# Starting the first batch's key projection on pieces of the context, with new engine orders, in a gated cross-attention and quantised feed-forward kernel

## The chip, the cores and the metric

The kernel runs on one core of one Trainium2 chip. The metric is the device time of one execution in microseconds. The kernel before takes 1027.44 us (median of 3 runs, 1027.41 to 1028.69).

## The reference

Sixteen batches of 224 rows of width 512 attend to 750 context rows of width 384 each, with 8 heads of 64, and then go through a quantised feed-forward layer of width 2048. All of it is in float32:

```python
h   = layernorm(x)
q, k, v = h @ W_q, context @ W_k, context @ W_v
sim = q k^T * 64**-0.5, masked keys set to the lowest float
x   = x + tanh(g_xattn) * (softmax(sim) @ v @ W_o + b_o)
z   = layernorm(x)
ffn(z): y = bitlinear(gelu(bitlinear(z, w1, b1)), w2, b2)
bitlinear(x, w, b) = act_quant(rmsnorm(x)) @ weight_quant(w).T + b
act_quant:    s = 127 / max|row|;  round(x s), clipped, / s
weight_quant: s = 1 / mean|w|;     round(w s) clipped to -1..1, / s
x   = x + tanh(g_ffn) * ffn(z)
```

The scale of each feed-forward weight is the mean of its absolute values, so no element of w2 or w1 can be quantised before all eight pieces of that matrix have been read and summed.

## The kernel before, in words

**Number formats.** A projection (keys, queries, values, output) is carried in float16 pairs: every operand is split into a high part (a cast) and a low part (the rest), and a product is three matmuls per contraction tile of 128 rows, high by high, low by high and high by low (`split_product`, line 770). ScalarE writes the high part of each result from PSUM and VectorE the low part. The feed-forward layer uses 8-bit weights.

**Banks.** PSUM has four banks for scores and `RING = 4` banks (`ps_g`) that all other products share in turn. The product with turn n goes to bank n % 4 and first waits (`need_bank`) until the product four turns before it has been emptied by its last reader, for keys the low part on VectorE.

**Orders by hand.** Each engine and the SyncE DMA queue works through a written list of steps, `SP_SEQ`, `PE_SEQ`, `ACT_SEQ`, `DVE_SEQ` and `POOL_SEQ` (lines 78 to 334). A step is `kind:n:batch`. An engine does its list strictly in order, and steps wait for each other through semaphores. The kinds that the text speaks of:

- `LX`, `LC`, `LM`, `LR` (SP): loads of a batch's x rows, of one third of its context (128 of 384 contraction rows by 750 keys), of its mask, and of residual rows of one tile. `LM` of a batch waits until the mask of the batch before has been turned into a bias (`MB`, POOL, line 1317).
- `PD`/`PW`: load of W_k, W_q, W_v, W_o (n = 0 to 3), then high part (ACT, line 1137) and low part (DVE, line 931). DVE's part releases TensorE through `wready`.
- `N1`, `XN`, `XH`: layer norm of x: statistics (DVE, lines 1013 and 1017), inverse root (POOL, lines 1323 and 1326), subtraction of the mean (DVE, line 1021, one instruction for each half of 112 rows), high part (ACT, line 1193) and low part (DVE, line 1025). `XT` is the DMA that transposes a half for the query projection.
- `CX`: high part (ACT, line 1199) and low part (POOL, line 1310) of one third of the context. The semaphore `ctx_lo` counts the low parts.
- `K:n` (PE, line 842): 8 key groups a batch, head pair n // 2, key half n % 2: 9 matmuls of 375 columns, 3 for each third. It begins after all three thirds: `need(pe, "ctx_lo", b, KC - 1)`. ACT copies (line 1174), DVE's `KL` (line 1000). `Q`, `V`: query and value groups, `QL`, `VL` on DVE.
- `S:n`: scores of 128 of the 896 rows; then for two units each `M` (DVE, mask and row minimum, line 978), `E` (ACT, exponential, line 1157), `R` (DVE), `N` (ACT, division, line 1162), `H` and `L` (POOL, casts, lines 1301 and 1306), `T` (transpose by DMA), `PV` (PE, line 826).
- `WL`, `WA`, `WS`, `WM`, `WB`, `WQ`: the feed-forward weights, 16 pieces: load, sum of absolute values (ACT, line 1147), their sum (DVE, line 958), the sum over partitions (PE, line 783, and DVE, line 947), scaling (POOL, line 1290), clipping (DVE, line 965). Pieces 0 to 7 are w2, 8 to 15 w1. This work is spread over the first 140 us.
- `O`, `L2`, `L3`, `L4`, `XQ`, `F1`, `GE`, `GS`, `GM`, `G2`, `G3`, `HT`, `F2`: output projection and feed-forward layer of a 128-row tile.

For batch 0 the lists of before begin like this:

```
PE   K:0 K:1 K:2 K:3 Q:0 Q:1 S:0 V:0 Q:2 S:1 K:4 K:5 S:2 V:1 V:2 V:3 S:3 K:6 V:4 V:5 K:7 S:4 Q:3 WM:0 S:5
ACT  PW:0 CX:0 CX:1 XH:0 CX:2 XH:1 PW:1 PW:2 K:0 K:1 K:2 K:3 Q:0 WA:0 Q:1 WA:1 E:0
DVE  N1 PW:0 XN XH:0 XH:1 PW:1 KL:0 KL:1 PW:2 QL:0 KL:2 KL:3 QL:1 M:0 M:1
POOL N1 CX:0 CX:1 CX:2 MB H:0 H:1 L:0 L:1
SP   PD:0 LX LC:0 LC:1 LC:2 PD:1 PD:2 XT:0 WL:0 XT:1 LM WL:1 WL:3 LM(batch 1) WL:5 LX(batch 1) ...
```

Of the kernel before, what the change touches and what calls it, by code (L numbers as in the profile page):

```python
# [17 lines left out]
HT = TQ // 2  # L18
# [3 lines left out]
CH = J // 2  # L22
# [50 lines left out]
def in_order(text):  # L73
# [10 lines left out]
    LC:2:3 XT:1:3 T:1:2 T:0:2 T:3:2 XQ:0:1 T:2:2 LC:1:4 T:4:2 LC:0:4 T:5:2 F2:1:0 LM:0:3 XQ:1:1 T:6:2 LR:1:2 T:7:2
    T:8:2 HT:0:1 T:9:2 LR:0:2 T:11:2 T:12:2 T:10:2 T:13:2 HT:1:1 LC:2:4 T:0:3 LX:0:5 F2:0:1 T:1:3 XT:1:4 XT:0:4
    XQ:0:2 F2:1:1 T:2:3 T:3:3 LR:0:3 T:4:3 T:6:3 LM:0:4 T:5:3 XQ:1:2 T:7:3 T:8:3 T:9:3 LC:0:5 HT:0:2 LR:1:3 T:11:3
    LC:1:5 T:12:3 T:10:3 T:13:3 LC:2:5 LX:0:6 XT:0:5 LM:0:5 XT:1:5 F2:0:2 HT:1:2 T:0:4 XQ:0:3 T:2:4 T:1:4 LR:1:4
    T:3:4 T:4:4 XQ:1:3 F2:1:2 T:5:4 T:6:4 T:7:4 HT:0:3 LC:1:6 T:8:4 LC:0:6 T:9:4 T:10:4 T:11:4 LX:0:7 T:13:4 T:12:4
# [15 lines left out]
    T:2:13 LM:0:14 T:3:13 T:4:13 F2:1:11 XQ:1:12 T:5:13 LR:1:13 LC:0:15 T:6:13 T:7:13 T:9:13 T:8:13 LM:0:15 T:11:13
    T:10:13 T:12:13 T:13:13 XT:0:15 HT:1:12 LC:2:15 T:0:14 T:1:14 F2:1:12 T:2:14 T:3:14 XQ:0:13 T:5:14 T:4:14
    XT:1:15 T:6:14 LR:0:14 T:7:14 XQ:1:13 HT:0:13 T:8:14 T:9:14 LR:1:14 T:11:14 T:10:14 T:13:14 T:12:14 F2:0:13
    LR:0:15 T:0:15 T:1:15 T:2:15 HT:1:13 T:3:15 XQ:0:14 T:4:15 F2:1:13 T:5:15 T:6:15 T:7:15 T:8:15 LR:1:15 T:9:15
    T:10:15 HT:0:14 T:11:15 T:12:15 T:13:15 F2:1:14 F2:0:14 F2:0:15 F2:1:15
# [351 lines left out]
def build(nc, x_d, ctx_d, mask_d, gx_d, gf_d, wq_d, wk_d, wv_d, wo_d, bo_d, w1_d, b1_d, w2_d, b2_d, out_d):  # L460
    with ExitStack() as stack:
# [937 lines left out]
```

## Time and profile before

| | |
|---|---|
| median of 3 runs | 1027.44 us |
| the profiled execution | 1028.62 us, of which its span (first to last instruction) 1026.7 us |
| TensorE (PE) busy | 977.3 us, 95% |
| ScalarE (ACT), VectorE (DVE), GpSimd (POOL) busy | 860.0, 800.2, 779.3 us |
| DMA queue of SyncE | 83.5% of 16 engines' span |
| mean granted TensorE clock | 0.989 |

The profile counts an engine as busy while it executes. A matmul's end is modelled, so TensorE's busy time is not the time at its peak, but its idle time is time in which it had nothing it could start. A timeline row gives start, length, engine, source line, operation, what it writes and reads, how many instructions are merged, and in brackets the idle time of the engine just before with what released it.

### The profile page before, as it was taken

To read this page: it belongs to the slowest core of one execution; us is meant where nothing else is said; L and a number is where in the kernel's file an instruction comes from. 1 tells how busy PE (TensorE), PEld (TensorE's weight loads), DVE (VectorE), ACT (ScalarE), POOL (GpSimd) and SP (SyncE) were. 2 spreads that over 40 slices of the span, in tenths; PEclk is the share of its full clock that TensorE was granted. 3 is DMA by queue.
4 is the path that set the end of the run, shared out by engine and by line. 5 is a ranking of instruction groups with operands and counts; after the bars stand their busy time and mean duration, and the time that the engine had idled before them with its cause. 6 is when DMAs were issued, how large, how long until landed. Compare 5 with 4: busy or idle time off the path is not lost.

```text
span 1026.7 us, 25406 instructions
## 1 busy us (share of the span) xinstructions
PE 977.3 (95%) x9216; PEld 562.0 (55%) x9216; DVE 800.2 (78%) x1870; ACT 860.0 (84%) x1386; POOL 779.3 (76%) x739
## 2 busy tenths in 40 slices
PE   3979898999999999999999999999999999999887
PEld 2536555565555656555555555555565556556443
DVE  6669788868998677977769778877868776876766
ACT  4879777988879879897888889798897977889866
POOL 3599998787678787877678696877687688867861
PEclk9989999999999999999999999999999999999989
DMA  6999979997879988978879798897888888778961
GB/s 229 239 212 244 206 159 157 177 163 135 189 142 173 187 168 157 169 130 172 155 153 172 157 187 162 137 174 142 169 163 182 166 167 153 138 133 162 168 100 41
DMA packets 472331, 169.10 MB, mean 165 GB/s; under 512 B 450320, under 2 KB 452368, under 8 KB 471824
## 3 DMA queue, kind: packets, MB, share of 16 engines
q1 hardware_dynamic: 472208, 167.48, 83.5%
q8 instruction: 75, 1.23, 0.5%
q14 instruction: 48, 0.39, 0.1%
HBM read 48.28 MB, written 7.34 MB: 54 GB/s over the span
## 4 chain that ended last, share of the span: by engine, by line
PE 68%; DVE 9%; POOL 6%; ACT 6%; DMA 5%; issue 4%; SPq 1%; DVEq 0%; POOLq 0%; ACTq 0%
PE ps_g L776 38%; PE ps_g L826 9%; PE ps_s L809 8%; PE ps_g L864 8%; PE ps_g L901 5%; POOL p L1306 3%; DMA pt<-p 2%; DVE xa L1021 2%; DVE prob L978 1%; POOL ctx L1310 1%; POOL p L1301 1%; ACT prob L1157 1%; ACT prob L1162 1%; DVE xc L1047 1%; ACT h_sb L1255 1%
## 5 line engine op out<-in xcount | busy, mean ns | idle before, releaser
L1306 POOL TENSOR_TENSOR p<-prob,p 128x750 f16<-128x750 f32 x224 | 357.8, 1608 | 4.8
L1301 POOL CAST p<-prob 128x750 f16<-128x750 f32 x224 | 186.0, 835 | 125.7 <-ACT prob L1162 100.1
L978 DVE CUSTOM_DVE_ANT_0 prob<-ps_s,mbias 128x750 f32<-128x750 f32 x224 | 205.8, 933 | 51.3 <-PE ps_s L809 35.2
L1157 ACT ACTIVATE prob<-prob,rmin 128x750 f32<-128x750 f32 x224 | 204.5, 914 | 26.2 <-DVE rmin L978 25.3
L1162 ACT ACTIVATE prob<-prob,rrec 128x750 f32<-128x750 f32 x224 | 198.7, 914 | 29.5 <-DVE rrec L923 29.3
L776 PE MATMUL ps_g<-ctx,wk 128*128 128x375 f16 x1152 | 201.1, 327 | 18.1 <-POOL ctx L1310 17.4
L776 PE MATMUL ps_g<-wv,ctx 128*128 128x512 f16 (+1 forms) x864 | 198.3, 379 | 1.2 <-DVE k_sb L1000 0.6
L776 PEld LDWEIGHTS ps_g<-ctx,wk 128*128 128x128 f16 x1152 | 110.9, 99 | 100.9 <-issue 29.6
L776 PEld LDWEIGHTS ps_g<-wv,ctx 128*128 128x128 f16 (+1 forms) x864 | 86.4, 103 | 97.3 <-issue 6.5
L809 PE MATMUL ps_s<-k_sb,q_sb 64*32 64x375 f16 (+2 forms) x2688 | 129.4, 325 | 7.7 <-DVE k_sb L1000 4.4
L826 PE MATMUL ps_g<-pt,v_sb 128*64 128x224 f16 (+2 forms) x2448 | 121.6, 256 | 4.5 <-DMA pt<-p 4.1
L826 PEld LDWEIGHTS ps_g<-pt,v_sb 128*64 128x64 f16 x2448 | 109.3, 111 | 23.0 <-issue 16.6
L864 PE MATMUL ps_g<-w,xqt 128*128 128x512 fp8e4 x432 | 103.6, 384 | 3.6 <-ACT xqt L1218 2.0
L901 PE MATMUL ps_g<-w,hqt 128*128 128x512 fp8e4 x432 | 97.7, 379 | 3.1 <-DMA hqt<-hq 2.4
L809 PEld LDWEIGHTS ps_s<-k_sb,q_sb 64*32 64x32 f16 (+2 forms) x2688 | 62.4, 95 | 65.5 <-issue 40.2
L1310 POOL TENSOR_TENSOR ctx<-ctx_f,ctx 128x750 f16<-128x750 f32 x47 | 74.1, 1585 | 17.8 <-ACT ctx L1199 17.3
L1075 DVE SCALAR_TENSOR_TENSOR h_sb<-ps_g,sm,b 128x512 f32<-128x512 f32 x108 | 76.8, 744 | 11.3 <-PE ps_g L864 10.7
L994 DVE SCALAR_TENSOR_TENSOR v_sb<-ps_g,v_sb 128x512 f16<-128x512 f32 x96 | 64.9, 685 | 24.3 <-ACT v_sb L1187 23.9
L776 PE MATMUL ps_g<-xt,wq 128*128 128x224 f16 x768 | 82.1, 259 | 0.7 <-DVE wv L931 0.4
L1000 DVE SCALAR_TENSOR_TENSOR k_sb<-ps_g,k_sb 128x375 f16<-128x375 f32 x128 | 67.8, 542 | 18.2 <-ACT k_sb L1174 18.0
L776 PEld LDWEIGHTS ps_g<-xt,wq 128*128 128x128 f16 x768 | 71.9, 98 | 12.9 <-issue 5.3
L776 PE MATMUL ps_g<-wo,attn 128*128 128x512 f16 x336 | 76.7, 380 | 1.3 <-DVE attn L988 1.3
(129 smaller groups left out, 1328.6 us busy)
## 6 DMA issues: line engine op xcount, KB each, us to landing
ctx_f<-in_ctx SPq DMA_DIRECT2D x47, 375.0 KB, 4.0
xa<-in_x SPq DMA_DIRECT2D x16, 448.0 KB, 4.7
xr<-in_x SPq DMA_DIRECT2D x28, 256.0 KB, 3.4
out<-xr SPq DMA_DIRECT2D x28, 256.0 KB, 2.9
pt<-p SPq DMA_TRANSPOSE x254, 4.1
h_sb<-in_w SPq DMA_DIRECT2D x4, 512.0 KB, 5.7
w<-in_w SPq DMA_DIRECT2D x3, 512.0 KB, 6.1
xr<-in_w SPq DMA_DIRECT2D x3, 512.0 KB, 5.0
```

The costliest lines, as they stand in the source:

```text
L776: mm = nc.tensor.matmul(out, lhs, rhs, start=(m == 0), stop=(m == len(steps) - 1))
L809: mm = nc.tensor.matmul(ps_s[at:at + width, e, c, 0:CH], q_sb[rows, j, qa, q:q + width], k_sb[rows, j, ka, c * CH:(c + 1) * CH], start=(m ...
L826: mm = nc.tensor.matmul(g[e * DH:(e + 1) * DH, 0:size], v_sb[:, p, t, va, (2 * j + e) * DH:(2 * j + e + 1) * DH], pt[:, e, pa * NT + t, pl ...
L864: mm = nc.tensor.matmul(g[:, :], xqt_t[:, k, :], w1v[:, k, f * 512:(f + 1) * 512], start=(k == 0), stop=(k == KD - 1))
L901: mm = nc.tensor.matmul(g[:, :], hqt_t[:, k, :], w2v[:, k, :], start=(k == 0), stop=(k == KF - 1))
L978: nc.vector.tensor_tensor_reduce(prob[:, (b * NU + n) % PROBS, :].rearrange("p (c k) -> p c k", c=2), ps_s[:, n % 2, :, 0:CH], mbias[:, :] ...
L1075: nc.vector.scalar_tensor_tensor(out=h_t[:, f * 512:(f + 1) * 512], in0=g[:, :], scalar=sm2[:, t % 2, 4:5], in1=b1[:, f * 512:(f + 1) * 51 ...
L1157: nc.scalar.activation(prob[:, (b * NU + n) % PROBS, :], prob[:, (b * NU + n) % PROBS, :], ACT.Exp, bias=rmin[:, n:n + 1], scale=-1.0, acc ...
L1162: nc.scalar.activation(held, held, ACT.Copy, scale=rrec[:, n:n + 1]).then_inc(normed, 1)
L1301: nc.gpsimd.tensor_copy(p16[:, u % HILO, 0, 0:J], prob[:, u % PROBS, :]).then_inc(hi_pool, 1)
L1306: nc.gpsimd.tensor_tensor(p16[:, u % HILO, 1, 0:J], prob[:, u % PROBS, :], p16[:, u % HILO, 0, 0:J], ALU.subtract).then_inc(lo_pool, 1)
L1310: nc.gpsimd.tensor_tensor(ctx[:, 1, n, :], ctx_place(b * KC + n), ctx[:, 0, n, :], ALU.subtract)\
```

## The change

Three things change.

**1. Key groups 0 to 3 of batch 0.** `K:0` now waits for one third of the context at a time. For the first two thirds it issues that third's three matmuls for each of the four groups, each into its own bank, and for the last third those of group 0. `K:1` to `K:3` issue the last third's three matmuls of their group. Number and shapes of the matmuls are as before.

```diff
+                elif kind == "K" and b == 0 and n < RING:
+
+                    for k in range(KC) if n == 0 else (KC - 1,):
+                        if n == 0:
+                            need(pe, "ctx_lo", b, k)
+                        for m in (n,) if k == KC - 1 else range(RING):
+                            j, c2 = m // 2, m % 2
+                            for a, c in ((0, 0), (1, 0), (0, 1)):
+                                mm = nc.tensor.matmul(bank(kind, m, b)[:, 0:CH], wk[:, a, k, j * 128:(j + 1) * 128],
+                                                      ctx[:, c, k, c2 * CH:(c2 + 1) * CH], start=(k == a == c == 0),
+                                                      stop=(k == KC - 1 and c == 1))
+                    mm.then_inc(s["k_proj"], 1)
```

**2. Two waits on VectorE**, both in the first feed-forward tile (t = 0):

```diff
                     need_tile(dve, "xq", t - 1)
+                    if t == 0:
+                        dve.wait_ge(w_abs, 2 * NW)
                     nc.vector.tensor_scalar(xc[:, :], xr_t, mv2[:, c, 0:1], None, ALU.subtract)\
...
                     need_tile(dve, "x2_amp", t)
+                    if t == 0:
+                        need(dve, "w_mean", 0, 1)
                     nc.vector.tensor_scalar(sm2[:, c, 4:5], sm2[:, c, 3:4], 1.0 / (QMAX * UNIT * W_UNIT), wmean[:, 0:1],
```

The first is there because `WA` writes its scratch output over `xc`, which `L2` writes.

**3. All five lists** have the same steps in another order: 371 of 464 places hold another step in SP's, 386 of 654 in PE's, 857 of 1035 in ACT's, 872 of 1071 in DVE's and 505 of 656 in POOL's, in every batch. For batch 0 they now begin:

```diff
-PE   K:0 K:1 K:2 K:3 Q:0 Q:1 S:0 V:0 Q:2 S:1 K:4 K:5 S:2 V:1 V:2 V:3 S:3 K:6 V:4 V:5 K:7 S:4 Q:3 WM:0 S:5
+PE   K:0 K:1 K:2 K:3 Q:0 Q:1 S:0 Q:2 V:0 S:1 K:4 K:5 S:2 V:1 V:2 V:3 K:6 V:4 V:5 K:7 S:3 S:4 Q:3 WM:0 S:5
-ACT  PW:0 CX:0 CX:1 XH:0 CX:2 XH:1 PW:1 PW:2 K:0 K:1 K:2 K:3 Q:0 WA:0 Q:1 WA:1 E:0
+ACT  PW:0 CX:0 XH:0 XH:1 CX:1 CX:2 PW:1 K:0 K:1 PW:2 K:2 K:3 Q:0 WA:0 Q:1 WA:1 E:0
-DVE  N1 PW:0 XN XH:0 XH:1 PW:1 KL:0 KL:1 PW:2 QL:0 KL:2 KL:3 QL:1 M:0 M:1
+DVE  PW:0 N1 XN XH:0 XH:1 PW:1 KL:0 KL:1 KL:2 KL:3 QL:0 PW:2 M:0 M:1 QL:1
-POOL N1 CX:0 CX:1 CX:2 MB H:0 H:1 L:0 L:1
+POOL CX:0 N1 CX:1 CX:2 MB H:0 L:0 H:1 L:1
-SP   PD:0 LX LC:0 LC:1 LC:2 PD:1 PD:2 XT:0 WL:0 XT:1 LM WL:1 WL:3 LM' WL:5 LX' LC:0' WL:2 LC:1' WL:7 T:0 WL:4 T:1 WL:6
+SP   PD:0 LX LC:0 LC:1 LM LC:2 PD:1 PD:2 XT:0 XT:1 WL:0 WL:1 LM' WL:2 LX' WL:5 WL:3 PD:3 WL:7 WL:4 LC:0' T:0 LC:1' WL:6 T:1
```

(a prime marks a step of batch 1). Where the sum of w2's absolute values is awaited and batch 1 begins:

```diff
-ACT  ... N:5 WA:4 WA:5 E:6 K:6 CX:0' K:7 WA:6 V:4 WA:7 XH:0' Q:3 XH:1' V:5 CX:1' E:7 E:8 E:9 CX:2'
+ACT  ... N:5 V:5 CX:0' WA:5 CX:1' WA:6 WA:7 E:6 E:7 K:7 Q:3 XH:1' CX:2' E:8 E:9
-DVE  ... KL:6 VL:4 WS:0 M:8 WM:0 XH:0' XH:1' M:9 QL:3 VL:5 KL:7
+DVE  ... KL:6 M:8 WS:0 M:9 WM:0 R:3 QL:3 XH:0' KL:7 XH:1'
-POOL ... CX:0' L:5 WB:0 CX:1' WB:1 CX:2' H:6 WB:2 WB:3 L:6
+POOL ... CX:0' H:5 CX:1' L:5 WB:0 WB:1 CX:2' WB:2 H:6 L:6
```

Around the new waits DVE's list read `O:1 QL:3 WS:1 L2:1 WM:1 R:3 M:8` and reads `O:1 L2:1 R:3 QL:3 WS:1 WM:1 KL:0 M:8`.

## Rows read from the trace of the kernel before

**Rows 1.** Stretches of the whole run: busy us (instructions) by engine, granted clock, DMA
```profile
core 0: us, PE busy (x) PEld busy (x) DVE busy (x) ACT busy (x) POOL busy (x), PEclk, DMA share, GB/s
0.00:50.00 50.00, 33.80 (x270) 18.73 (x270) 33.31 (x57) 33.58 (x56) 24.06 (x30) 1.00 0.84 235
50.00:62.00 12.00, 4.36 (x67) 2.45 (x64) 7.27 (x21) 12.00 (x21) 10.62 (x8) 0.76 0.92 227
62.00:108.00 46.00, 45.53 (x438) 27.94 (x436) 38.18 (x78) 38.13 (x75) 45.56 (x36) 0.95 1.03 228
108.00:162.00 54.00, 47.78 (x506) 29.20 (x504) 45.93 (x104) 41.64 (x74) 50.52 (x45) 1.00 0.90 171
162.00:960.00 798.00, 793.07 (x7450) 456.50 (x7451) 629.71 (x1510) 687.48 (x1094) 615.59 (x588) 1.00 0.86 161
960.00:1027.00 67.00, 52.76 (x494) 27.18 (x492) 45.78 (x103) 47.19 (x70) 32.97 (x37) 0.91 0.46 91
```

**Rows 2.** Timeline of all engines from 5 to 31 us (start, length)
```profile
5.32 1.48 ACT L1137 ACTIVATE wk<-xr 128x1536 f16<-128x1536 f32 x1 [3.32 <-DMA xr<-in_wk]
6.81 1.29 DVE L1013 BATCH_NORM_STATS2 st<-xa 112x6 f32<-112x512 f32 x2 [5.96 <-DMA xa<-in_x]
7.65 1.80 ACT L1199 ACTIVATE ctx<-ctx_f 128x750 f16<-128x750 f32 x2 [0.84 <-DMA ctx_f<-in_ctx]
...
8.23 1.73 DVE L931 SCALAR_TENSOR_TENSOR wk<-xr,wk 128x1536 f16<-128x1536 f32 x1
8.40 1.60 POOL L1323 TENSOR_SCALAR ve<-mv 112x2 f32<-112x2 f32 x1 [4.92 <-DVE mv L1017]
9.87 6.05 DVE L1021 TENSOR_SCALAR xa<-xa,mv 112x512 f32<-112x512 f32 x2
...
10.90 3.17 POOL L1310 TENSOR_TENSOR ctx<-ctx_f,ctx 128x750 f16<-128x750 f32 x2
...
15.79 7.31 PE L776 MATMUL ps_g<-ctx,wk 128*128 128x375 f16 x36 [15.79 <-POOL ctx L1310]
...
15.96 0.72 ACT L1193 ACTIVATE xh<-xa,rs 112x512 f16<-112x512 f32 x1 [3.48 <-DVE xa L1021]
...
16.59 1.89 ACT L1137 ACTIVATE wq<-h_sb 128x2048 f16<-128x2048 f32 x1
...
18.51 2.29 DVE L931 SCALAR_TENSOR_TENSOR wq<-h_sb,wq 128x2048 f16<-128x2048 f32 x1 [1.05 <-ACT wq L1137]
18.56 4.15 PEld L776 LDWEIGHTS ps_g<-ctx,wk 128*128 128x128 f16 x26 [0.17 <-issue]
...
19.76 0.98 ACT L1174 ACTIVATE k_sb<-ps_g 128x375 f16<-128x375 f32 x2
...
20.72 1.00 DVE L1000 SCALAR_TENSOR_TENSOR k_sb<-ps_g,k_sb 128x375 f16<-128x375 f32 x2
...
23.51 2.46 PE L776 MATMUL ps_g<-xt,wq 128*128 128x224 f16 x24 [0.41 <-DVE wv L931]
...
25.90 1.13 PE L809 MATMUL ps_s<-k_sb,q_sb 64*128 64x375 f16 x12
...
26.39 0.83 POOL L1317 TENSOR_SCALAR mbias<-mask 128x750 bf16<-128x750 uint8 x1 [10.75 <-DMA mask<-in_mask]
...
30.52 0.57 ACT L1187 ACTIVATE v_sb<-ps_g 128x512 f16<-128x512 f32 x1
```

**Rows 3.** Timeline of TensorE from 52 to 67 us
```profile
53.74 0.38 PE L783 MATMUL ps_g<-wsum,xqt 128*128 128x1 f32 x2 [1.93 <-DVE wsum L958]
58.51 2.08 PE L809 MATMUL ps_s<-k_sb,q_sb 64*32 64x375 f16 x48 [4.39 <-DVE k_sb L1000]
61.74 5.34 PE L776 MATMUL ps_g<-ctx,wk 128*128 128x375 f16 x18 [1.15 <-POOL ctx L1310]
```

**Rows 4.** Line 1021 from 100 to 1000 us: ns of one, min/median/max
```profile
L1021 DVE TENSOR_SCALAR xa<-xa,mv x26: 474/943/3606, 149.7 to 853.7; 112x512 f32<-112x512 f32 x26
```

**Rows 5.** DMA issues from 18.5 to 19.8 us, us from issue to landing
```profile
xt<-xh SPq DMA_TRANSPOSE x1, 4.8
```

**Rows 6.** The page's costliest groups: the exponential, busy us, mean ns
```profile
L1157 ACT ACTIVATE prob<-prob,rmin 128x750 f32<-128x750 f32 x224 | 204.5, 914 | 26.2 <-DVE rmin L978 25.3
```

More of the change, by code:

```diff
@@ L84 @@
[L84 to L88, printed above, removed]
@@ L104 @@
[L104 to L108, printed above, removed]
+    PD:0:0 LX:0:0 LC:0:0 LC:1:0 LM:0:0 LC:2:0 PD:1:0 PD:2:0 XT:0:0 XT:1:0 WL:0:0 WL:1:0 LM:0:1 WL:2:0 LX:0:1 WL:5:0
@@ new lines @@
+    T:2:11 T:3:11 LR:0:11 LC:1:13 LC:0:13 XQ:1:10 T:4:11 T:5:11 T:6:11 T:7:11 T:8:11 T:9:11 HT:0:10 T:10:11 T:11:11
+    T:12:11 T:13:11 LX:0:14 XT:0:13 LR:1:11 LM:0:13 XT:1:13 LC:2:13 T:0:12 T:1:12 T:2:12 HT:1:10 XQ:0:11 T:4:12
+    F2:0:10 T:3:12 T:5:12 XQ:1:11 T:7:12 LC:1:14 LR:1:12 T:8:12 T:6:12 LC:0:14 T:9:12 HT:0:11 T:10:12 T:11:12
+    T:13:12 T:12:12 LX:0:15 LC:2:14 LM:0:14 HT:1:11 T:0:13 T:1:13 F2:1:10 T:2:13 XT:1:14 T:3:13 XT:0:14 T:5:13
+    T:4:13 T:6:13 XQ:1:12 T:7:13 T:8:13 LC:0:15 F2:0:11 T:9:13 LR:1:13 T:10:13 F2:1:11 T:11:13 T:12:13 T:13:13
@@ L147 @@
[L147 to L151 removed]
+    K:0:0 K:1:0 K:2:0 K:3:0 Q:0:0 Q:1:0 S:0:0 Q:2:0 V:0:0 S:1:0 K:4:0 K:5:0 S:2:0 V:1:0 V:2:0 V:3:0 K:6:0 V:4:0
@@ new lines @@
+    N:12:2 N:13:2 GE:1:1 PL:1:2 V:4:3 E:0:3 K:5:3 K:6:3 GS:1:1 E:1:3 V:5:3 XH:0:4 XH:1:4 K:7:3 N:0:3 N:1:3 CX:0:4
+    CX:1:4 E:2:3 G3:1:1 E:3:3 PL:2:2 PL:3:2 N:2:3 N:3:3 Q:3:3 CX:2:4 E:4:3 E:5:3 E:6:3 E:7:3 N:4:3 N:5:3 L4:0:2
+    E:8:3 Q:0:4 V:0:4 V:1:4 E:9:3 N:6:3 N:7:3 N:8:3 GE:0:2 E:10:3 K:0:4 L4:1:2 K:1:4 K:2:4 N:9:3 E:11:3 PL:0:3
+    GS:0:2 K:3:4 V:2:4 E:12:3 N:10:3 V:3:4 E:13:3 Q:1:4 K:4:4 G3:0:2 N:11:3 N:12:3 N:13:3 E:0:4 E:1:4 K:5:4 PL:1:3
+    XH:0:5 GE:1:2 N:0:4 V:4:4 N:1:4 K:6:4 XH:1:5 K:7:4 CX:0:5 CX:1:5 V:5:4 Q:2:4 E:2:4 E:3:4 N:2:4 PL:2:3 PL:3:3
@@ new lines @@
+    PL:1:10 V:4:11 N:0:11 E:2:11 V:5:11 CX:0:12 K:6:11 GS:1:9 K:7:11 E:3:11 N:1:11 N:2:11 N:3:11 CX:1:12 PL:2:10
+    PL:3:10 CX:2:12 Q:2:11 G3:1:9 E:4:11 Q:3:11 K:0:12 E:5:11 N:4:11 L4:0:10 E:6:11 E:7:11 V:0:12 N:5:11 E:8:11
+    E:9:11 N:6:11 L4:1:10 N:7:11 K:1:12 N:8:11 GE:0:10 V:1:12 V:2:12 GS:0:10 XH:0:13 XH:1:13 Q:0:12 Q:1:12 K:2:12
+    E:10:11 PL:0:11 E:11:11 V:3:12 N:9:11 N:10:11 K:3:12 K:4:12 N:11:11 K:5:12 G3:0:10 E:12:11 E:13:11 N:12:11
+    N:13:11 E:0:12 E:1:12 PL:1:11 V:4:12 GE:1:10 N:0:12 V:5:12 N:1:12 K:6:12 GS:1:10 K:7:12 Q:2:12 Q:3:12 E:2:12
@@ new lines @@
+    F1:5:10 R:6:11 M:0:12 M:1:12 F1:6:10 R:0:12 F1:7:10 M:2:12 M:3:12 PA:1:11 VL:4:12 VL:5:12 XH:0:13 XH:1:13
+    KL:6:12 KL:7:12 QL:2:12 QL:3:12 M:4:12 M:5:12 R:1:12 GM:1:10 M:6:12 PA:2:11 PA:3:11 G2:1:10 R:2:12 F2:0:10
+    N1:0:14 O:0:11 L2:0:11 O:1:11 QL:0:13 M:7:12 L3:0:11 XN:0:14 R:3:12 L2:1:11 VL:0:13 QL:1:13 KL:0:13 M:8:12
+    M:9:12 F2:1:10 L3:1:11 F1:0:11 F1:1:11 R:4:12 F1:2:11 KL:1:13 F1:3:11 PA:0:12 M:10:12 M:11:12 GM:0:11 G2:0:11
+    KL:2:13 M:12:12 KL:3:13 R:5:12 M:13:12 VL:1:13 VL:2:13 VL:3:13 R:6:12 KL:4:13 M:0:13 F1:4:11 F1:5:11 F1:6:11
@@ L334 @@
+    L:4:15 XB:0:15 L:5:15 H:6:15 H:7:15 L:6:15 H:8:15 L2:1:14 L:7:15 L:8:15 H:9:15 L:9:15 G2:0:14 H:10:15 H:11:15
+    L:10:15 L3:1:14 L:11:15 H:12:15 H:13:15 L:12:15 L:13:15 L2:0:15 XB:1:15 G2:1:14 L2:1:15 G2:0:15 G2:1:15 L3:0:15
+    L3:1:15
 """)
```

457 lines of the change are left out of this document (221 added, 236 removed).

## The prediction

> **What bounds the kernel now.** I first read the stretches of the whole run [rows 1], because every list changes and the question is where TensorE can still be given time. TensorE is the bound: over the 798 us from 162 to 960 us it is idle for 798.00 - 793.07 = 4.9 us in all, at full clock, and no other engine is near that. Its idle time is at the two ends: 16.2 us up to 50 us, 7.6 us from 50 to 62, 0.5 us from 62 to 108, 6.2 us from 108 to 162, and about 14 us after 960. So time that is won before 62 us is kept only if the stretch from 62 to 162 lets it through. From 62 to 108 TensorE has no slack, so it passes a lead on if its inputs come earlier too. But GpSimd is full there (45.56 of 46 us) and so is the DMA (share 1.03), so a lead of TensorE alone would become a wait.
>
> Then I read the timeline of the start [rows 2]. TensorE waits 15.79 us, for GpSimd's low part of the last third of the context. The 36 key matmuls take 7.31 us from there. Of their 36 weight loads 26 come from 18.56 on in 4.15 us, 0.16 us apart; the 10 before them took 2.8 us, about 0.31 apart after the first pair. That is 375 columns at 1.2 and then at 2.4 GHz, after an engine that had done nothing so far (the granted clock's column says 1.00 for the whole stretch, so here I go by the spacing). The other chain of the start is x: the two mean subtractions take 6.05 us together. Then come both high parts, W_q's split, and the first query group at 23.51. Scores follow at 25.90, and the row minimum waits for the mask's bias, which GpSimd writes at 26.39 after 10.75 us of waiting for a mask load that stood late in the DMA list.
>
> Third, the stall at 50 to 62 [rows 3]. TensorE waits 1.93 us for the sum of w2's absolute values, 4.39 for a key group's low part queued behind other work on ScalarE and VectorE, 1.15 for batch 1's context. ScalarE is busy 12.00 of the 12 us [rows 1], so this stall is a matter of what stands ahead of what on ScalarE. TensorE's clock falls in it: 0.76 for the stretch, and the next 18 key matmuls take 5.34 us where 18 take half of about 5.9 us at full clock.
>
> **Part 1: the start.** Removed: the wait for all three thirds. Walking the new lists with the durations of [rows 2]:
> - VectorE has W_k's low part first: ready at 6.80, 1.64 us (the row less the overlap), done 8.45. Statistics 1.29 + 0.2: done 9.95.
> - GpSimd has the first third first: its high part is there at 8.46, 1.6 us, done 10.1. TensorE can start at 10.1 instead of 15.8.
> - Mean subtractions from 9.95. Before, they took 6.05 us while GpSimd was at work without a pause from 8.40 to 15.65; elsewhere one takes 0.47 to 3.61 us, median 0.94 [rows 4]. Now GpSimd has two small instructions and then nothing until ScalarE gives it the second third, which stands behind both `XH`. So I take 1.6 us for the pair. Bounds: 0.9 and the old 6.05.
> - Both `XH` on ScalarE (0.72 each) from 11.5 to 12.9, then both `CX` (0.9 each): 13.8 and 14.6. GpSimd: second third 13.7 to 15.3, last third to 16.9. That is 1.2 us later than before for the last third, the price of putting x first.
> - TensorE: 12 matmuls from 10.1, cold for the most part, 3.5 us, done 13.6; wait to 15.3; 12 at 0.16 to 17.3; 12 to 19.2. Bounds for the last 24: 0.16 each (3.8 us) or 0.31 each (7.4 us) if the pause costs the clock. I take the first, because in [rows 3] the pauses before the clock fell were longer (1.93 and 4.39 us).
> - x transposes: first at 13.0, second issued by 14.4, landing 4.8 us later [rows 5]: 19.2.
> - W_q: ScalarE 14.6 to 16.5, VectorE 2.29 from 16.9 (it waits for GpSimd's last third, see below): 19.2. Before: 20.80. Key low parts 0.5 each after it, so bank 0 is free at 19.7 and `Q:0` starts there, 3.8 us earlier than 23.51. ScalarE puts W_v's high part (three quarters of 1.89, 1.4 us) ahead of `K:2`, and VectorE does four `KL` before `QL:0`: done 22.3. `S:0` then starts at 22.3 instead of 25.90: 3.6 us earlier.
> - The mask's load moves ahead of `LC:2`. It delays the last third's load by one issue, about 0.5 us, which `XH` covers, since `CX:2` now runs at 13.7. The bias is ready long before `S:0`, and the next batch's mask load, x load and five weight loads, queued behind that bias at 27.2, go out some 6 us sooner.
>
> From here to the stall TensorE has work without gaps, and of its order little but the place of `S:3` differs, so the lead is **3.6 us** if ScalarE and VectorE empty the banks as before.
>
> For the mean subtractions the trace shows this too: GpSimd's variance instruction of 2 columns took 1.60 us during VectorE's W_k split [rows 2]. The Trainium skill (SBUF — State Buffer, Who interferes with whom) has it that VectorE's two-port modes, and VectorE instructions with two SBUF inputs, share a port pair with GpSimd under an exclusive lock. The trace agrees with 1.60 and 6.05 us. By that rule the pair of subtractions would cost about 1 us once GpSimd idles, 0.6 less than I take, and the start of `XH` would move by as much; the sum does not use it.
>
> **Part 2: the stall at 50 to 62.** ScalarE's list up to `WA:7` has the same steps as before less `E:6` and `K:7`, plus `V:5`, `XH:0` and `CX:1` of batch 1: -0.91 [rows 6] -0.49 +0.57 +0.72 +0.9 [rows 2] = +0.8 us. So `WA:7` and TensorE's `WM:0` come 3.6 - 0.8 = 2.8 us earlier. Loads do not hold it, as they go out sooner. Behind it stand `E:6 E:7 K:7 Q:3` (0.91 + 0.91 + 0.49 and, for 224 columns, some 0.4: 2.7 us), then VectorE's `QL:3`, `XH:0`, `KL:7` (0.4, 0.7 and 0.5 like their high parts): `KL:7` ends 4.3 us after `WA:7`. Before it was 4.9 (53.6, just ahead of `WM:0`, to 58.5 [rows 3]). `S:5` is 3.4 us earlier. Batch 1's last third: GpSimd had `WB CX WB CX` after the mean and has `WB WB CX`, one subtraction of 1.6 us less. So `K:0` of batch 1 starts 2.8 + 1.6 = 4.4 us earlier, at 57.3. **Lead 4.3 us** at the end of the stall, for TensorE and for GpSimd alike, so the full stretch up to 108 can pass it on. The low clock stays, since the wait before `S:5` is nearly as long as before.
>
> **Part 3: 62 to 162.** The same steps, GpSimd still full. One thing helps: `CX:2` of batch 2 stands one `L` earlier. One thing can hurt: DVE's `L2:1` now waits for `WA:15`, with `R:3` and `QL:3` behind it. But `QL:3` needs ScalarE's `Q:3`, which itself stands behind `WA:15`, and `R:3` is late by one weight sum at most. I cost it at nothing; what hides it is ScalarE's order. If that cover failed, N:6 and through it GpSimd would be late by about 1.5 us once. The wait for `w_mean` is met long before. Value 0, bounds -3 (half of the 6.2 us idle) and +2 (half of the lead lost).
>
> **Part 4: the other 13 batches.** At most 4.9 us of idle to gain in 800 us, so every reordering there can only lose more than it gains. No row shows what a new order does. Bounds: -2, and +4, if as much idle again is made as there is now. I take 0, near the present state.
>
> **Part 5: the last 67 us**, 14 us idle, mostly waits of the last two tiles, whose order in PE's list is nearly the same. Value 0, bounds -1.5 and +1.5.
>
> **Sum.** -4.3, rounded to -4.2 for a start that hangs on several landings. Against the profiled execution's own 1028.62 that is 1024.4. That execution is 1.2 us above the median of the three runs, so against 1027.44 the forecast is **1023.2 us**.
>
> **The rivals.**
> - *A, the forecast* (0.50): the lead of 4.3 us goes through. 1021.3 to 1025.3.
> - *B, the pieces bring little* (0.12). Either the pause of 1.7 us costs the clock (24 matmuls by 0.15 = 3.7 us), or the subtractions stay long and hold `XH` and with it `CX:1` on ScalarE, which is now behind them (4.4 us). The key groups then end at about 23, and only the GpSimd order of part 2 is left of the gain: 1027.44 - 0.8 = 1026.6. For it: the 6.05 us. Against it: GpSimd is idle then.
>  The Trainium skill (TensorE: Matmul & The Clock Gate, Part 1) says that the array's clock halves after idleness and recovers only after sustained work. This trace agrees at 15.79 and at 58.51. By that rule the pause alone could give B; the 0.12 comes from the lengths of the pauses in [rows 3], not from it.
> - *C, the lead is half absorbed* (0.15) between 62 and 162, where DMA and GpSimd are full. For it: both at capacity. Against: both start their share earlier. 1027.44 - 2 = 1025.4.
> - *D, the new orders also close gaps* (0.14): 3 us of the 6.2 and 1 of the 4.9. 1019.2.
> - *E, slower* (0.09): lists in the steady state that hold TensorE. Places moved furthest are `XH:1` of batch 12 (25 and 28 places earlier on ScalarE and VectorE), where ScalarE waits in order for the layer norm and the free transpose buffer, and exponentials queue behind. The steady part has 13 batches; at 0.5 us more idle in each it costs 6.5 us, more than the lead, and gives 1029.7. It decides once idle from 162 to 960 passes 4.9 + 4.3 = 9.2 us.
>
> **How the numbers follow.** About 2 us, 0.2%, is what a measurement of this kernel tells from no change: faster is below 1025.4, slower above 1029.5. Faster: nearly all of A, D, half of C: 0.71. Same: the rest of C, B: 0.20. Slower: E: 0.09. The range 1019.0 to 1027.6 holds A, B, C and part of D, and leaves out E and the far part of D.
>
> **What would show it.** Key matmuls at about 10.1, in three groups with a pause before the second; both subtractions under 2.5 us; `Q:0` near 19.7; `S:0` near 22.3; `WM:0` near 51; batch 1's keys near 57.3; TensorE's idle from 162 on near 5 us again. The forecast is wrong if the lead at batch 1's keys is under 2 us (part 1 or 2), or if it is there and idle after it has grown (parts 3 to 5).

## The result: slower, and where the time went

The changed kernel takes **1036.14 us** (median of 4 runs, 1034.13 to 1036.61), the kernel before 1027.43 beside it (4 runs, 1027.35 to 1028.69): the ratio is 1.007, 95% interval 1.0053 to 1.0086. The forecast was 1023.2 with a range to 1027.6. So the change costs some 9 us where a gain of 4 was expected. The profiled execution took 1036.61, of which the span is 1034.8 us.

I read the same stretches first as before the change. Stretches of the changed kernel, columns as in [rows 1]:

```profile
0.00:50.00 50.00, 33.63 (x258) 18.22 (x258) 32.02 (x57) 35.20 (x59) 25.85 (x31) 1.00 0.91 254
50.00:62.00 12.00, 7.44 (x81) 4.53 (x82) 9.92 (x25) 11.80 (x20) 11.26 (x8) 0.57 0.99 224
62.00:108.00 46.00, 41.68 (x379) 24.80 (x379) 33.51 (x65) 32.00 (x62) 37.96 (x31) 0.89 0.78 188
108.00:162.00 54.00, 50.79 (x530) 31.14 (x528) 47.91 (x108) 43.69 (x77) 52.50 (x46) 1.00 0.95 183
162.00:960.00 798.00, 786.82 (x7407) 454.24 (x7402) 629.73 (x1497) 684.77 (x1094) 614.53 (x584) 1.00 0.85 160
960.00:1027.00 67.00, 56.99 (x550) 29.39 (x548) 52.56 (x121) 51.70 (x76) 38.95 (x43) 0.92 0.55 104
```

Two rows stand out. From 62 to 108 us GpSimd is busy 37.96 us where it had 45.56 [rows 1]: the full stretch that was to pass the lead on has holes in it. And from 162 to 960 TensorE is idle 798.00 - 786.82 = **11.2 us** where it was 4.9. The prediction named 9.2 us as the point from which rival E decides.

Then I set both executions side by side at equal work: for each of TensorE's steps its start now less its start before. This is worked out from the two timelines:

```
step (start before, us)      start now less start before, us
first key group  (15.8)      -5.1
S:0              (25.9)      -3.5
at 43                        -3.7
at 52                        +0.1
K:0 of batch 1   (61.7)      -1.7
at 79                        -1.5
at 90                        +4.4
at 238                       +1.2
at 288                       +5.9
at 440                       +7.6
at 956                       +9.1
```

The start did what it was to do. Most of the loss is made in four stretches: 43 to 52, 79 to 90, 238 to 288 and 288 to 440. Between the second and the third, 3.2 us of it come back. The timeline of the start, changed kernel:

```profile
10.31 0.87 DVE L1033 TENSOR_SCALAR xa<-xa,mv 112x512 f32<-112x512 f32 x2
10.65 3.77 PE L845 MATMUL ps_g<-ctx,wk 128*128 128x375 f16 x12 [10.65 <-POOL ctx L1326]
15.65 4.00 PE L845 MATMUL ps_g<-ctx,wk 128*128 128x375 f16 x24 [1.24 <-POOL ctx L1326]
19.88 2.46 PE L776 MATMUL ps_g<-xt,wq 128*128 128x224 f16 x24 [0.22 <-issue]
22.36 0.81 PE L809 MATMUL ps_s<-k_sb,q_sb 64*128 64x375 f16 x8
```

The keys start at 10.65 (forecast 10.1), the query at 19.88 (19.7) and the scores at 22.36 (22.3). Now the four stretches. TensorE of the changed kernel, the rows that end a long wait (in brackets its length and what ended it):

```profile
45.55 1.61 PE L776 MATMUL ps_g<-ctx,wk 128*128 128x375 f16 x9 [2.48 <-DVE v_sb L1006]
...
50.25 1.14 PE L809 MATMUL ps_s<-k_sb,q_sb 64*128 64x375 f16 x12 [2.01 <-DVE rmin L990]
...
56.40 2.08 PE L809 MATMUL ps_s<-k_sb,q_sb 64*32 64x375 f16 x48 [2.71 <-DVE k_sb L1012]
60.08 2.35 PE L776 MATMUL ps_g<-ctx,wk 128*128 128x375 f16 x7 [1.60 <-POOL ctx L1326]
...
84.64 1.61 PE L776 MATMUL ps_g<-ctx,wk 128*128 128x375 f16 x9
90.56 3.00 PE L776 MATMUL ps_g<-ctx,wk 128*128 128x375 f16 x9 [4.32 <-DVE v_sb L1006]
...
275.61 1.74 PE L776 MATMUL ps_g<-ctx,wk 128*128 128x375 f16 x9 [3.04 <-DVE k_sb L1012]
...
429.74 0.60 PE L876 MATMUL ps_g<-w,xqt 128*128 128x512 fp8e4 x2 [1.51 <-DVE xr L1139]
```

At 45.55, 90.56, 275.61 and 429.74 TensorE waits for VectorE to empty a bank. The wait at 90.56 costs its clock too: nine matmuls take 3.00 us where the nine before took 1.61, and the granted clock of the stretch is 0.89. What VectorE does just before is a mean subtraction (`XN`, now line 1033), and before 429.74 the layer norm's centring (`L2`, line 1061). VectorE of the changed kernel in the four places:

```profile
39.92 4.97 DVE L1033 TENSOR_SCALAR xa<-xa,mv 112x512 f32<-112x512 f32 x2
44.81 1.27 DVE L1006 SCALAR_TENSOR_TENSOR v_sb<-ps_g,v_sb 128x512 f16<-128x512 f32 x2
...
83.48 4.71 DVE L1033 TENSOR_SCALAR xa<-xa,mv 112x512 f32<-112x512 f32 x2
...
268.44 6.33 DVE L1033 TENSOR_SCALAR xa<-xa,mv 112x512 f32<-112x512 f32 x2
...
424.11 2.98 DVE L1061 TENSOR_SCALAR xc<-xr,mv 128x512 f32<-128x512 f32 x1
```

A pair takes 4.97, 4.71 and 6.33 us; at 10.31 it took 0.87, and there GpSimd had only the last 0.2 us of a context third and two small instructions of 2 columns. GpSimd at the same times, changed kernel:

```profile
41.14 3.08 POOL L1322 TENSOR_TENSOR p<-prob,p 128x750 f16<-128x750 f32 x2
...
84.84 3.07 POOL L1322 TENSOR_TENSOR p<-prob,p 128x750 f16<-128x750 f32 x2
...
269.46 4.63 POOL L1322 TENSOR_TENSOR p<-prob,p 128x750 f16<-128x750 f32 x3
...
423.63 3.18 POOL L1322 TENSOR_TENSOR p<-prob,p 128x750 f16<-128x750 f32 x2
```

GpSimd's instructions there end at 44.22, 87.91, 274.09 and 426.81 us. Each time the one instruction that was held ends 0.28 us later; the other subtraction of the pair takes 0.47 to 0.73. This is theory **P** (port): a subtraction that meets GpSimd at work is held, here through one to three more of GpSimd's instructions, and behind it in VectorE's list stands the eviction that frees TensorE's next bank. At 429.74 the chain is longer (the centring, then a maximum and a row minimum before the eviction), and no run tested this place in the changed orders.

Not every subtraction is held so long. Of the 64 in the two profiles 57 meet a GpSimd instruction that is running. 50 of these wait at most for that one instruction (49 end 0.28 to 0.35 us after it, one before it) and take at most 1.83 us, even where GpSimd's next one follows without a pause:

```profile
149.74 1.59 DVE L1033 TENSOR_SCALAR xa<-xa,mv 112x512 f32<-112x512 f32 x1
```
```profile
149.53 1.51 POOL L1322 TENSOR_TENSOR p<-prob,p 128x750 f16<-128x750 f32 x1
150.99 1.01 POOL L1317 CAST p<-prob 128x750 f16<-128x750 f32 x1
```

The subtraction ends at 151.33, inside GpSimd's run. The other seven are passed over by one to three more GpSimd instructions and take 1.57 to 5.94 us. What decides between the two is open.

The old order had long pairs too, in other places (6.05 us at the start, where TensorE waited for the context anyway), and the sum over all 32 is nearly equal, 39.7 us before and 40.4 now. So no table of busy time shows it; only the place does.

For line 1033 from 100 to 1000 us the median is 1026 ns and the longest 5937, where [rows 4] has 943 and 3606:

```profile
L1033 DVE TENSOR_SCALAR xa<-xa,mv x26: 473/1026/5937, 149.7 to 854.3; 112x512 f32<-112x512 f32 x26
```

### The profile page after: what moved, and what is told of

Read it like the earlier page. It is cut to its first block, busy times and chain, and to the rows that moved or that the text cites. A ratio compares the mean times of both kernels' runs of the same rounds, so it can differ in the third digit from the quotient of the medians.

```text
span 1034.8 us, 25408 instructions
## 1 busy us (share of the span) xinstructions
PE 981.5 (95%) x9216; PEld 564.2 (55%) x9216; DVE 807.2 (78%) x1870; ACT 861.1 (83%) x1386; POOL 781.0 (75%) x739
## 4 chain that ended last, share of the span: by engine, by line
PE 64%; DVE 11%; POOL 9%; ACT 7%; issue 5%; DMA 3%; SPq 1%; DVEq 0%; POOLq 0%; ACTq 0%
PE ps_g L776 35%; PE ps_s L809 8%; PE ps_g L826 7%; PE ps_g L876 7%; PE ps_g L913 6%; POOL p L1322 3%; POOL p L1317 2%; DVE xa L1033 2%; POOL ctx L1326 2%; ACT prob L1173 2%; DVE prob L990 1%; DVE xc L1061 1%; DMA pt<-p 1%; ACT prob L1178 1%; SPq L740 1%
## 5 line engine op out<-in xcount | busy, mean ns | idle before, releaser
L776 PE MATMUL ps_g<-ctx,wk 128*128 128x375 f16 x1116 | 197.1, 329 | 11.9 <-DVE v_sb L1006 6.8
L776 PEld LDWEIGHTS ps_g<-ctx,wk 128*128 128x128 f16 x1116 | 107.9, 99 | 93.3 <-issue 14.9
```

The source lines that it names most:

```text
L776: mm = nc.tensor.matmul(out, lhs, rhs, start=(m == 0), stop=(m == len(steps) - 1))
```

## The experiments

They ran on three chips: 1 to 4 on one, 5 to 8 on the second, 9 to 12 on the third. The kernel before took 1029.87, 1029.33 and 1029.79 us there (medians of 13, 22 and 11 runs), 2 us more than beside the result above. Each ratio is to the kernel before on the same chip, and across chips only ratios are compared. The expectations call the first form of the subtraction two-port and the form of experiment 1 one-port or accumulating.

**1 and 2. The mean subtraction in another form, in both kernels.** The same arithmetic with a running sum as second output, which nobody reads. All lists stay as they are.

```
-  nc.vector.tensor_scalar(xa[:, half, :], xa[:, half, :], mv1[:, half, 0:1], None,
-                          ALU.subtract).then_inc(s["x_cent"], 1)
+  nc.vector.tensor_scalar(xa[:, half, :], xa[:, half, :], mv1[:, half, 0:1], 0.0,
+                          ALU.subtract, ALU.add,
+                          accum_out=xsum[:, 2 * b + half:2 * b + half + 1])
+      .then_inc(s["x_cent"], 1)
```

> The changed kernel with one instruction in another form: the two mean subtractions of each batch (XN) also write the sum of their result to a scratch column. All lists stay as changed. Theory P (port): in the changed kernel XN of batches 1, 2 and 5 lasted 5.0, 4.7 and 6.3 us because GpSimd was at work without a pause, and the bank that TensorE waited for was emptied behind them; in this form VectorE does not share a port with GpSimd, so every pair takes about 1.3 us, the gaps of 2.5, 4.3 and 3.0 us before K:7 of batch 0, K:5 of batch 1 and K:6 of batch 4 vanish with the clock that they cost, and the time falls from 1036.1 to about 1026 (1023 to 1030). Theory O (order): XN only happened to be there, the lists starve the banks anyway; then the pairs get short and the time stays above 1033.

> The kernel before with the same other form of XN and nothing else. Its XN of batch 0 took 6.1 us and set the start of the query projection. Theory P: that pair takes 1.3 us, but Q:0 still waits for W_q's low part (VectorE) and the keys, so the start gains at most 2 us; the long pairs of batches 12 and 1 (4.0 and 2.8 us) delayed nobody. 1024 to 1027.5. Theory O expects the same here, 1027. If XN's length mattered nowhere, exactly 1027.4.

Measured: the changed kernel 1023.39 us, ratio 0.9933 (0.9914 to 0.9952); the kernel before 1023.85, ratio 0.9939 (0.9920 to 0.9958). The instruction in the changed kernel of experiment 1 (min/median/max ns):

```profile
L1034 DVE TENSOR_SCALAR_CACHE_REDUCE xa<-xa,mv x32: 729/741/746, 10.0 to 840.0; 112x512 f32<-112x512 f32 x32
L1034 DVE DVE_READ_ACCUMULATOR xa<-xa,mv x32: 81/83/88, 10.7 to 840.6; 112x1 f32 x32
```

All 32 take the same time now, whatever GpSimd does. TensorE in the same kernel around the first two places:

```profile
42.50 1.60 PE L777 MATMUL ps_g<-ctx,wk 128*128 128x375 f16 x9
...
50.86 0.45 PE L784 MATMUL ps_g<-wsum,xqt 128*128 128x1 f32 x2
54.03 1.56 PE L810 MATMUL ps_s<-k_sb,q_sb 64*32 64x375 f16 x48 [2.72 <-issue]
57.71 2.67 PE L777 MATMUL ps_g<-ctx,wk 128*128 128x375 f16 x8 [2.12 <-POOL ctx L1329]
...
81.37 3.05 PE L777 MATMUL ps_g<-ctx,wk 128*128 128x375 f16 x18
```

The waits of 2.48 and 4.32 us are gone, and so is that of 3.04 at batch 4's K:6. The wait for a row minimum stays (2.01 us before 50.25, here 2.00 before 47.19), and so does the one behind the layer norm's centring, which keeps its form. VectorE and TensorE of experiment 1:

```profile
411.23 2.98 DVE L1064 TENSOR_SCALAR xc<-xr,mv 128x512 f32<-128x512 f32 x1
```
```profile
416.85 1.04 PE L877 MATMUL ps_g<-w,xqt 128*128 128x512 fp8e4 x4 [1.89 <-DVE xr L1142]
```

The form itself gives the kernel before 6 us, just more than I had written, and most of the gain comes bit by bit between 200 and 750 us. What matters for the change: **with this form both orders take the same time** (0.9933 and 0.9939); with the two-port form they differ by 0.8% (experiment 5). So the difference between the orders goes away with the held subtractions. That the reason is a shared port is the theory's part; what the runs show is that the length varies in one form and not in the other.

**3. The pieces alone.** The changed code for the first four key groups, with all five lists of the kernel before.

> The piece-wise K:0 alone, with all five lists of the kernel before. GpSimd's first third is there at 12.5 us, so TensorE starts 3.3 us earlier and the keys end near 20. Theory X (x binds next): Q:0 still waits for the x transpose, issued at 18.6 and landed 4.8 us later, so it starts at 23.3 as before and the time is 1027.4 within 0.5. Theory K (keys bind): Q:0 starts near 21.3 and the time is 1025.5.

Measured: 1030.84 us, ratio 1.0009 (0.9991 to 1.0026). TensorE and VectorE of experiment 3 at the start:

```profile
12.89 7.93 PE L853 MATMUL ps_g<-ctx,wk 128*128 128x375 f16 x36 [12.89 <-POOL ctx L1334]
23.62 1.64 PE L784 MATMUL ps_g<-xt,wq 128*128 128x224 f16 x9 [2.80 <-DVE wv L951]
```
```profile
10.11 6.05 DVE L1041 TENSOR_SCALAR xa<-xa,mv 112x512 f32<-112x512 f32 x2
```

TensorE starts 2.9 us earlier and waits 2.80 us before the query. The profile names W_v's low part as the last to come, which `Q:0` does not wait for (it needs W_q's); in experiment 10, with the same start, it names the transpose of x (2.86 us). So x is the chain that binds as soon as the context doesn't, as theory X had it, and x is late by the 6.05 us pair. The pieces bring nothing without the order that puts x first.

**4. The start alone.** The changed code with the changed orders up to 31.8 us of the changed kernel's execution (SyncE's up to `WL:4:0`), the orders of before from there.

> Pieces plus the new lists up to 31.8 us of the changed kernel's execution (batch 0 up to the third scores, SP up to WL:4), then every list in the order of before. Theory P: the lead of 3.6 us at S:0 is real and is lost only later by where XN stands in the new lists; here S:0 starts at 22.4 and the lead of 3 to 4 us reaches the end: 1023.5 to 1025. Theory L (a lead cannot be carried): it is lost between 30 and 60 us in ScalarE's full stretch whatever the lists are, and the time is 1027 or more.

Measured: 1025.33 us, ratio 0.9955 (0.9938 to 0.9971): the start is worth 4.5 us here. Its subtraction pairs of batches 1, 2 and 5 take 2.8, 2.7 and 2.6 us. TensorE of experiment 4 at the start:

```profile
10.72 3.92 PE L853 MATMUL ps_g<-ctx,wk 128*128 128x375 f16 x12 [10.72 <-POOL ctx L1334]
15.78 5.73 PE L853 MATMUL ps_g<-ctx,wk 128*128 128x375 f16 x24 [1.14 <-POOL ctx L1334]
```

After a pause of 1.14 us the 24 matmuls took 5.73 us; after 1.24 us in the changed kernel they took 4.00. In experiment 4 the first twelve weight loads come 0.31 us apart and the last twelve 0.16, in the changed kernel all at about 0.16. The prediction's two spacings both occur, so the clock in this pause is not decided by its length alone. It cost experiment 4 part of its lead at first: `S:0` starts at 24.21 and not at 22.4 as expected. By the scores at 70.90 of the kernel before the lead is 3.9 us, and about 3 us of it are there at the end of this execution. That is theory P and not L.

**5. The changed kernel again**, as a control on this chip.

> The changed kernel as it is, a control on the chip of the other experiments. 0.6 to 0.9% over the kernel before, and with it 1.2 to 1.6% over the same lists with the mean subtraction without its two-port form.

Measured: 1039.11 us (1031.36 to 1043.26, 10 runs), ratio 1.0078 (1.0052 to 1.0103). This ratio and that of experiment 1 lie 1.5% apart, from the form of one instruction. In its profile the pair at 80 us takes 8.30 us, and TensorE waits 6.91:

```profile
79.99 8.30 DVE L1033 TENSOR_SCALAR xa<-xa,mv 112x512 f32<-112x512 f32 x2
```
```profile
90.66 3.00 PE L776 MATMUL ps_g<-ctx,wk 128*128 128x375 f16 x9 [6.91 <-DVE v_sb L1006]
```

**6. Three pairs moved back.** The instructions and everything else as in the changed kernel.

```
VectorE: XN:0:1 behind VL:5:0, XN:0:2 behind VL:3:1, XN:0:5 behind PA:1:3
ScalarE: XH:0:1 behind V:5:0,  XH:0:2 behind N:13:0, XH:0:5 behind GE:1:2
```

> The changed kernel with three of its 16 pairs of mean subtractions (batches 1, 2 and 5) a few steps further back on VectorE, behind the eviction that TensorE waits for, and the matching XH:0 behind V:5:0, N:13:0 and GE:1:2 on ScalarE. The instructions are the same. Theory P (VectorE in its two-port form waits for GpSimd, and what stands behind it empties TensorE's banks): the waits of 2.5 us before K:7:0, 4.3 before K:5:1 and 3.0 before K:6:4 go or fall under 1 us each, and the time falls from 1036 to between 1027 and 1031. Theory O (it is the number of such overlaps, wherever they stand, or TensorE is late for other reasons): the pairs stay as long, the time stays above 1033.

Measured: 1032.37 us, ratio 1.0024 (1.0001 to 1.0047), 6.7 us less than experiment 5. That is between what I wrote for P and for O, whose numbers assumed the 1036 of the first result. The waits before K:7 and K:6:4 are gone and that before K:5:1 is 0.24 us. But one of the three moves only moved its wait. ScalarE and TensorE of experiment 6:

```profile
88.12 1.33 ACT L1214 ACTIVATE xh<-xa,rs 112x512 f16<-112x512 f32 x2 [5.54 <-DVE xa L1038]
```
```profile
94.63 1.89 PE L781 MATMUL ps_g<-wv,ctx 128*128 128x512 f16 x4 [5.66 <-DVE attn L1005]
```

In batch 2 the subtraction is now late for ScalarE, which stands 5.54 us in `XH:0:2` with `K:4:1` and `PL:1:0` (the high part of a weighted-value product) behind it, and TensorE waits 5.66 us for the bank of `PL:1:0`. So moving a pair recovers what its bank wait cost only where ScalarE's list lets it.

**7. The changed orders up to 162 us**, those of before from there (SyncE's from `T:12:2`).

> The changed kernel's orders up to 162 us on each engine, the orders of before from there on. Theory P with the trace (the changed kernel is 1 to 2 us behind before at 162 us, 8 us at its end, and 6 of these 8 are two long subtractions at 268 and 423 us): 1028 to 1031. Theory S (the loss is made before 162 us, in the state of DMA and GpSimd that the first batches leave behind): 1033 to 1037.

Measured: 1043.3 us (1039.03 to 1046.42), ratio 1.0128 (1.0084 to 1.0172). It is above both ranges and tells less than it was to. At 200.5 us TensorE waits 5.30 us for a row minimum, and that for GpSimd, which had stood 8.01 us waiting for a transpose of SyncE's. Neither kernel has this wait: my seam lies at 162 us on four engines and near 200 on SyncE.

**8. The changed start with the one-port subtraction.** Experiment 4 and experiment 1's edit together.

> The changed start up to 31.8 us, the order of before from there, and the mean subtraction in its accumulating form without two ports. If the gain of the start (-4.5 beside before on this chip) and of the subtraction (-6.0) are independent, they add up to 1019 to 1020 beside 1029.9; if both take the same idle time of TensorE out, 1023 to 1024.

Measured: 1021.70 us (7 runs, 1018.43 to 1025.12), ratio 0.9923 (0.9897 to 0.9949). Between the two expectations; the two gains add only in part.

**9 and 10. A clean seam.** Near 226 us both kernels have done the same set of steps on each of the five engines. Experiment 9 has the changed orders up to it and those of before behind it, experiment 10 the other way round.

> The changed kernel's orders up to a seam near 226 us, the orders of before from there. The seam is where both kernels have done the same set of steps on each engine, so no step changes sides. Theory P (each list has its own few places where a two-port VectorE instruction meets a run of GpSimd's): the first 226 us cost 2 to 3 us as in the changed kernel, nothing after: 1031 to 1033 beside 1029.5. Theory S (a late start of GpSimd and DMA spoils what follows, whatever the order): 1036 or more.

> The orders of before up to the same seam near 226 us, the changed kernel's from there; the context still goes in pieces. Theory P: the long subtractions at 268 (6.3 us) and 423 us (4.6 us) come back, although TensorE is not late at 226 us: 1034 to 1038, where the same with all orders of before had 1030.8. Theory S: at 1031, as there.

Measured: experiment 9 takes 1040.18 us, ratio 1.0105 (1.0091 to 1.0120), outside P's numbers and by them a point for S. In its profile TensorE is 4.3 us behind at the seam; then comes one wait of 5.65 us, 6 us behind the seam, for a query bank that VectorE empties late; from there to 960 us it stays at 9.6 to 11.1 us behind. So the orders of before don't go on losing when they start late, which speaks against S as written, but the seam costs something of its own again, and the total can't be used. Experiment 10 takes 1036.17 us, ratio 1.0067 (1.0049 to 1.0086), as P had it, where the same code with all orders of before has 1.0009 (experiment 3). VectorE and TensorE of experiment 10:

```profile
266.68 5.93 DVE L1041 TENSOR_SCALAR xa<-xa,mv 112x512 f32<-112x512 f32 x1
```
```profile
273.84 1.45 PE L784 MATMUL ps_g<-ctx,wk 128*128 128x375 f16 x8 [3.03 <-DVE k_sb L1020]
```

TensorE comes to the seam 0.4 us behind before, and yet the long subtraction and the wait of 3.03 us (3.04 in the changed kernel) are back. They belong to the order behind 226 us and not to what the first batches leave. The second one, of 423 us, which P expected too, did not come back, so the loss of 0.6% behind this seam is explained by one held subtraction only in part.

**11. Both centrings without two ports, orders of before.** The edit of experiment 1 on the layer norm's centring as well.

> The kernel before with both centrings (of the next batch's x and of the first layer norm) in the accumulating form without two ports. If the layer norm's centring costs TensorE something too (its pairs stand at 3 to 4 us now and then), 1020 to 1022 beside 1029.5; if it is hidden, 1023 to 1024 as with the first alone.

Measured: 1023.65 us, ratio 0.9941 (0.9925 to 0.9957), the same as experiment 2: in this order the layer norm's centring is hidden.

**12. The changed orders up to a seam near 57 us, both centrings without two ports.**

> The candidate for the best: the changed kernel's orders up to a seam near 57 us, the orders of before from there, both centrings without two ports. The changed start brings its 4.3 us of the prediction (it had 4.0 with the one-port subtraction), the subtraction 6.0: 1019 to 1020 beside 1029.5 if they add up, 1021.5 to 1023 if the low clock or the stretch after 62 us takes part of it back.

Measured: **1019.92 us** (6 runs, 1017.00 to 1023.58), ratio 0.9913 (0.9893 to 0.9933), as expected if the two gains add up. It is the lowest of all and faster than both kernels; from experiment 8 (0.9897 to 0.9949) it can't be told apart. TensorE is idle 798.00 - 794.02 = 4.0 us from 162 to 960. Stretch of experiment 12:

```profile
162.00:960.00 798.00, 794.02 (x7502) 458.77 (x7501) 623.19 (x1565) 691.64 (x1102) 615.54 (x594) 1.00 0.87 162
```

## Why the prediction was wrong

**Part 1 held.** Keys at 10.65, query at 19.88, scores at 22.36: the lead was 3.5 us at the scores where 3.6 was worked out. The subtraction pair took 0.87 us, the lower bound, and the pause did not cost the clock. Experiment 3 shows that the x chain, which the prediction walked beside the context, is the half that decides. By the rule of the Trainium skill (SBUF — State Buffer, Who interferes with whom), an exclusive lock on the shared port pair, the prediction put the pair at about 1 us with GpSimd idle; at 0.87 us, with GpSimd nearly idle, the trace agrees.

**The step that failed** is the condition at the end of part 1: TensorE has work without gaps "if ScalarE and VectorE empty the banks as before". They did not. The lead was -3.7 at 43 us and +0.1 at 52: a wait of 2.48 us for a value bank behind the pair at 39.92, and 2.01 for the row minimum at 50.25. The second comes from the new place of `S:3`, just ahead of `S:4`, which the prediction called little; experiment 1 has it too (2.00) and is still 4.0 us ahead at batch 1's keys, so it costs nothing that lasts. The first is where the condition fell. I had compared TensorE's order and ScalarE's order up to there and not VectorE's, where `XN:0:1` stands ahead of `VL:3:0` instead of behind `M:7:0`. The exclusive use of the port that I cited for the first pair applies to the other 15 as well; I priced it once, at the place where it had been long, and left the others at nothing. It was the rule that spoke against this change, and it should have been a term of parts 2 to 4.

**Part 2** came to 1.7 us at batch 1's K:0 instead of 4.3. Its sum itself was right: with the one-port form, so with the banks emptied as before, `WM:0` starts at 50.86 (forecast near 51) and batch 1's K:0 at 57.71 (forecast 57.3), 4.0 us ahead of 61.74.

**Part 3** was given 0 with a bound of +2. From 79 to 90 us alone it lost 5.9 us: 4.32 of wait and most of the rest at half clock, in the nine key matmuls (3.00 us for 1.61) and the scores behind it. Between 90 and 238 us 3.2 us come back, so by 238 us the part has cost 2.9 us net (-1.7 to +1.2), still outside its bound. The bound was half of the lead, as if only the lead could be lost. The wait I had looked at, `L2:1:0` for `WA:15`, cost nothing that shows in TensorE's waits.

**Part 4** was given 0 with bounds of -2 and +4. TensorE is idle 11.2 us there instead of 4.9, so it cost 6.3. Two places make most of it, 268 and 423 us; experiment 10 brings the first back alone. With the one-port form the changed orders still leave 798.00 - 790.54 = 7.5 us idle, against 798.00 - 794.65 = 3.4 for the orders of before in the same form. So about 4 us of part 4 do not come from the subtractions; they lie at the bound and cancel most of the start's lead: that is why experiments 1 and 2 take the same time. Their two profiled executions, set side by side at equal work, say more: experiment 1 is 4.6 us ahead of experiment 2 at 62 us, 5.1 at 400, 2.8 at 430 and 1.1 at 956. So over half of these 4 us are lost at one place, where the centring at 411.23 takes 2.98 us in its two-port form and TensorE waits 1.89 before 416.85. No run has the changed orders with both centrings in the one-port form all the way, so that this too is a held instruction is argued and not shown. The rest, 1.7 us, is open.

**Part 5** went as said: TensorE is 9.1 us late at 956 and the end is 8.1 us late (spans of 1034.8 and 1026.7).

**The rivals.** E was the right one, at 0.09, by its own criterion (11.2 us of idle against 9.2), but it gave 1029.7 for a small loss in every batch. In truth single places of 1.5 to 6 us each did most of it, two of them before 162 us, and the places E pointed at (`XH:1` of batch 12) have no wait of over 1.2 us near them. The range ended at 1027.6 because E was left out of it. A, C and D all rested on the one condition that fell. That E had the sign right is luck as far as its mechanism goes: it had ScalarE's list hold TensorE, and it was VectorE's.

**What stays open:** what makes a subtraction wait for one GpSimd instruction or for several, whether what the changed start brings can be kept with all changed orders behind it, and why seams at 162 and at 226 us each give a wait of 5 to 6 us.

## What to carry to other kernels

When a list of VectorE's steps is reordered, look in the timeline at every instruction whose time varies with what GpSimd does (here one line from 473 to 5937 ns) and ask for each what stands directly behind it and whether TensorE waits for that; its sum over the run may stay the same while the time moves by 0.8%. Where such an instruction can be had in a form of constant duration, even one that is slower at its best (741 + 83 ns against 473), take it before searching for an order: it made both orders 0.6% or more faster and nearly indifferent to their differences. And if a prediction rests on "as before", that clause needs its own row for every engine, and its failure belongs into the range.

## What the runs showed of the hardware that I had not expected

A subtraction in its two-port form that meets GpSimd is not slowed but held: it ends 0.28 to 0.35 us after the end of one of GpSimd's instructions (56 of 57 cases). In 49 that is the instruction it met, in seven it is a later one, and then the price is up to 5.94 us for one, and 8.30 for a pair in experiment 5. The Trainium skill (SBUF — State Buffer, Who interferes with whom) speaks of an exclusive lock; these rows agree with it, but for the seven the end of the instruction they met was not enough. The kernel before shows the same on an instruction with two SBUF inputs, the low part of x, which takes 4.11 us and ends at 272.69, 0.55 us after GpSimd's three instructions of 267.49 to 272.14; at 12.61 us of the changed kernel two of them take 1.42. VectorE and GpSimd of the kernel before:

```profile
268.58 4.11 DVE L1025 SCALAR_TENSOR_TENSOR xh<-xa,rs,xh 112x512 f16<-112x512 f32 x1
```
```profile
267.49 4.65 POOL L1306 TENSOR_TENSOR p<-prob,p 128x750 f16<-128x750 f32 x3
```

And two pauses of nearly the same length (1.14 and 1.24 us) before the same 24 matmuls left TensorE at 0.24 us for each on average in one kernel and at 0.17 in the other.
